# Groups in pairs with all batches inside a pair, in a grouped attention on one Trainium2 core

## The reference

```python
def _div_clamp_fp8(x, scale):
    y = jnp.clip(x.astype(jnp.float32) / scale, -FP8_MAX, FP8_MAX)
    y = y.astype(jnp.bfloat16).astype(jnp.float32)
    return _fp8_roundtrip(y)
...
ln_out = _ln(hidden_states, ln_w, ln_b)
q = _ln(_fp8_linear_pertensor(ln_out, wq, wq_scale, q_in_scale).reshape(b, s, g, hpg, d), qln_w, qln_b)
k = _ln(_fp8_linear_pertensor(ln_out, wk, wk_scale, k_in_scale).reshape(b, s, g, d), kln_w, kln_b)
v = _fp8_linear_pertensor(ln_out, wv, wv_scale, v_in_scale).reshape(b, s, g, d)
core = _gqa(q, k, v).reshape(b, s, nh * d)
qx = _ln(_fp8_linear_pertensor(ln_out, wqx, wqx_scale, qx_in_scale).reshape(b, s, g, hpg, d), qxln_w, qxln_b)
kx, vx = jnp.split(jnp.einsum('bsi,oi->bso', cond, w_kv_x), 2, axis=-1)
...
xout = _gqa(qx, kx, vx).reshape(b, s, nh * d)
catq = _div_clamp_fp8(jnp.concatenate([core, xout], axis=-1), proj_smooth)
return jnp.einsum('bsi,oi->bso', catq, wproj) * (proj_in_scale * proj_w_scale)
```

## Time and profile before

| | us |
|---|---|
| median of 3 runs (lowest, highest) | 987.29 (986.53, 988.27) |
| the profiled execution: its own time | 992.78 |
| its span | 991.0 |
| PE busy | 921.8 (93%) |
| DVE busy | 748.4 (76%) |
| ACT busy | 585.3 (59%) |
| POOL busy | 490.0 (49%) |

### The profile page before, as it was taken

One profiled execution on the slowest core, in us unless ns is written; L12 is line 12 of the kernel. 1 busy time (PEld: TensorE's weight loads), 2 busy tenths in 40 slices (PEclk: granted clock), 3 DMA queues, 4 the chain that ended last, 5 costly groups with the idle time before them and its releaser, 6 DMA issues. The chain is left out here.

```text
span 991.0 us, 17524 instructions
## 1 busy us (share of the span) xinstructions
PE 921.8 (93%) x5677; PEld 739.2 (75%) x5677; DVE 748.4 (76%) x2035; ACT 585.3 (59%) x1711; POOL 490.0 (49%) x409
## 2 busy tenths in 40 slices
PE   7999999998889988996889999999999999999988
PEld 6455656665768655664678899988999889999976
DVE  6764564433785778998899889789887898788785
ACT  1753444437435778864664766756766667766743
POOL 3265667652124223434666565475664755645650
PEclk9998999999999989997999999999999999999999
DMA  9725212214101200000020100101002010000201
GB/s 320 285 87 222 78 67 86 75 75 184 47 1 62 86 2 2 3 22 0 22 64 1 32 13 2 65 1 44 1 1 65 1 43 1 4 20 2 97 1 43
DMA packets 19657, 55.18 MB, mean 56 GB/s; under 512 B 3264, under 2 KB 9488, under 8 KB 19056
## 3 DMA queue, kind: packets, MB, share of 16 engines
q1 hardware_dynamic: 13968, 40.68, 11.4%
q0 software_dynamic: 4512, 12.33, 3.6%
q10 hardware_dynamic: 1088, 1.05, 0.3%
HBM read 45.78 MB, written 8.26 MB: 55 GB/s over the span
## 5 line engine op out<-in xcount | busy, mean ns | idle before, releaser
L2513 ACT ACTIVATE y<-bank,g_mx 128x256 f32<-128x256 f32 x256 | 117.2, 484 | 115.6 <-DVE g_mx L2696 115.6
L2797 POOL TENSOR_TENSOR y<-y,g_sm 128x1024 f32<-128x1024 f32 x64 | 119.9, 1893 | 25.3 <-DVE g_sm L2712 25.3
L2773 POOL TENSOR_TENSOR g_c<-arena 128x1024 fp32r<-128x1024 f32 x30 | 64.0, 2132 | 112.4 <-DVE arena L2617 112.4
L2386 PE MATMUL bank<-arena 128*128 128x256 f32 x512 | 116.3, 380 | 0.0
L2386 PEld LDWEIGHTS bank<-arena 128*128 128x128 f32 x512 | 94.9, 190 | 12.0 <-issue 0.2
L767 PE MATMUL bank<-arena 128*128 x188 | 90.0, 602 | 0.0
L2269 PE MATMUL bank<-cst,y 128*128 128x128 f32 x512 | 71.9, 274 | 10.9 <-POOL y L2797 6.3
L2696 DVE TENSOR_REDUCE g_mx<-bank 128x2 f32<-128x512 f32 x128 | 79.2, 675 | 0.2 <-PE bank L2386 0.2
L1105 DVE TENSOR_SCALAR arena<-bank 128x256 f32<-128x256 f32 x47 | 19.9, 423 | 76.5 <-PE bank L767 68.1
L2363 PE MATMUL bank<-g_qh,g_xs 128*128 128x256 f32 x256 | 66.8, 298 | 7.0 <-POOL g_xs L2747 6.8
L2305 PE MATMUL bank<-g_ph,g_c 128*128 128x256 f32 x248 | 65.9, 304 | 4.0 <-ACT y L2513 2.3
(11 more groups left out here) (427 smaller groups left out, 2656.2 us busy)
## 6 DMA issues: line engine op xcount, KB each, us to landing
arena<-in_dram SPq DMA_DIRECT2D x16, 768.0 KB, 15.4
arena<-in_dram SPq DMA_DIRECT2D x21, 512.0 KB, 3.7
arena<-b_pairs SPq DMA_DIRECT2D x8, 512.0 KB, 7.4
arena<-in_dram SPq DMA_DIRECT2D x3, 1024.0 KB, 5.0
arena<-in_dram SPq DMA_DIRECT2D x2, 704.0 KB, 5.6
x<-in_dram SPq DMA_DIRECT2D x4, 256.0 KB, 5.1
cx<-in_dram SPq DMA_DIRECT2D x4, 256.0 KB, 5.3
cxT<-in_dram SPq DMA_DIRECT2D x4, 256.0 KB, 5.8
```

What stands on the lines that cost most here:

```text
L2386: m = pe.matmul(o[:, st * 256:st * 256 + 256], g_t[:, c, st * P:st * P + P], keys, start=True, stop=True)
L2513: m = act.activation(g_p[:, c, st, :], o[:, st * 256:st * 256 + 256], ACT.Exp, bias=g_mx[j % 2][:, 2 * c + st:2 * c + st + 1], accum_out=g ...
L2773: pool.tensor_tensor(cat, g_o[j % 2], g_om, ALU.subtract).then_inc(s_gc, 1)
L2797: pool.tensor_tensor(pf, pf, sums, ALU.mult).then_inc(s_gp, 1)
```

## The change

The order of items becomes pairs of groups: items 0 to 7 are (g0, b0), (g1, b0), (g0, b1), (g1, b1), and so on, so that keys and values are projected in every even iteration, two buffers hold them in place of four, and batches finish one after the other in the last pair. The raw query weights get places of their own: the second group's are loaded and centred in the mLSTM stage already, later ones wait in part of yT and of the arena. The preparation for the next pair stands at iterations 5 to 8 of a pair: centring of the even group at the end of 5, of keys and of the odd group at the end of 6, the even group's splits at the end of 7 (ACT's high parts at its start, with those of keys and values), the low parts of keys and values early in the first iteration of the new pair, the odd group's splits at its end, and the projection's splits in the fourth and fifth. Roundings of batches 1 to 3 move to the ends of iterations 0 to 4. One buffer holds the quantised output in place of two. In the last layer, batches 0 and 1 are normalised in iterations 29 to 32, and PE does their transposes and logits around the last items; the lists of the feed-forward are reordered to match. Arena addresses shift by 48.

The diff, cut to its core:

```diff
                 if s_ == 3:
                     split_w_dve(dve, 0, BOTH)
+                    centre_w_dve(dve, V, 1)
...
+        PAIR = 2 * B
+        G_OF = [2 * (j // PAIR) + j % 2 for j in range(NG)]
+        B_OF = [j % PAIR // 2 for j in range(NG)]
...
-        g_o = [yT[:, i, :] for i in range(2)]
-        g_f = [arena[:, at_:at_ + 1024] for at_ in (19456, 11264, 18432, 16384)]
+
+        def g_o(j):
+
+            return yT[:, 1, :] if j == NG - 1 else yT[:, 0, :]
...
-        kv_at = [(arena[:, 35792:36304], arena[:, 36304:36816]), (arena[:, 36816:37328], arena[:, 37328:37840]),
-                 (kv_more[:, 0:512], kv_more[:, 512:1024]), (arena[:, 37840:38352], arena[:, 26624:27136])]
-        g_k, g_v = ([kv_at[b][n].rearrange("p (t g d) -> p t g d", t=2, g=2) for b in range(B)] for n in range(2))
+        kv_at = [(arena[:, 35840:36352], arena[:, 36352:36864]), (kv_more[:, 0:512], kv_more[:, 512:1024])]
...
-                   1: (("G", "yt", 3),) + CROSS[3]}
+        G_AHEAD = {0: CROSS[1]}
+        G_EXTRA = {0: (("F", "t", 2), ("F", "o", 2)) + CROSS[2][0:3] + (("F", "t", 3), CROSS[2][3], ("F", "o", 3)) + CROSS[3],
+                   1: (("G", "yt", 2), ("G", "yt", 3)),
...
-            at_ = 35792 if g == 0 else (13312, 15360)[g % 2]
-            return arena[:, at_:at_ + 1024].rearrange("p (k n) -> p k n", k=KD)
+            if g < 2:
+                raw = (arena[:, 35840:36864], kv_more[:, :])[g]
+            else:
+                raw = (yT[:, 1, :], arena[:, 26624:27648])[g % 2]
+            return raw.rearrange("p (k n) -> p k n", k=KD)
...
-            at_ = 36816 if p == 0 else 14336
-            return arena[:, at_:at_ + 1024].rearrange("p (k n) -> p k n", k=KD)
+            return arena[:, 36864:37888].rearrange("p (k n) -> p k n", k=KD)
...
             sp.dma_start(g_pr(0), wp_d[0]).then_inc(s_gwp, 16)
-            sp.wait_ge(s_gx, 12)
-            sp.dma_start(g_qr(1), wq_d[1]).then_inc(s_gw, 16)
-            sp.wait_ge(s_gx, 16)
+            sp.wait_ge(s_gx, 8)
+            sp.wait_ge(s_gwp, 16)
             sp.dma_start(g_pr(1), wp_d[1]).then_inc(s_gwp, 16)
-            for g in range(2, G):
-                last = B * (g - 2) + B - 1
-                take(sp, ("G", "q", last, 1))
-                sp.dma_start(g_qr(g), wq_d[g]).then_inc(s_gw, 16)
-                if g % 2 == 0:
-                    take(sp, ("G", "kv", last, 1))
-                    sp.dma_start(g_kr(g // 2), wkv_d[g // 2]).then_inc(s_kvw, 16)
-                take(sp, ("G", "pj", last))
-                sp.dma_start(g_pr(g), wp_d[g]).then_inc(s_gwp, 16)
+            for p in range(1, G // 2):
+                if p == 1:
+                    sp.wait_ge(s_gv1, 32)
+                else:
+                    sp.wait_ge(s_gwl, 4 * (2 * p - 1))
+                sp.dma_start(g_qr(2 * p), wq_d[2 * p]).then_inc(s_gw, 16)
+                if p == 1:
+                    sp.wait_ge(s_gx, 16)
+                else:
+                    sp.wait_ge(s_kvl, 4 * p)
+                    sp.wait_ge(s_gwl, 4 * (2 * p))
+                sp.dma_start(g_kr(p), wkv_d[p]).then_inc(s_kvw, 16)
+                sp.wait_ge(s_gw, 16 * (2 * p + 1))
+                sp.dma_start(g_qr(2 * p + 1), wq_d[2 * p + 1]).then_inc(s_gw, 16)
+                for g in (2 * p, 2 * p + 1):
+                    take(sp, ("G", "pj", PAIR * p - 2 + g % 2))
+                    sp.wait_ge(s_gwp, 16 * g)
+                    sp.dma_start(g_pr(g), wp_d[g]).then_inc(s_gwp, 16)
...
                 G_pv(pe, j, a, o)
+            H_logits_pe(pe, 1)
+            H_column_pe(pe, 0)
             o = claim(pe, ("G", "pj", j - 1))
             pe.wait_ge(s_gc, j)
             G_pj(pe, j - 1, o)
+            yt_pe(pe, K_H, "H", (2,))
...
                 if i < NG:
-                    g, b = i // B, i % B
...
                     if i == 0:
                         keep_busy(pe, claim(pe, ("G", "q", 0, 0)), 6)
                     if b == 0:
                         pe.wait_ge(s_gwl, 4 * (g + 1))
-                        if g % 2 == 0:
-                            pe.wait_ge(s_kvl, 4 * (g // 2 + 1))
-                    if i < B:
-                        pe.wait_ge(s_gx, 4 * i + 4)
+                    if i < PAIR and i % 2 == 0:
...
                     cross_v_pe(pe, 2, g_wvx[:, 0, :], g_wvx[:, 1, :], (3,))
                     F_o_pe(pe, 3)
+                    cross_v_pe(pe, 3, g_wvx[:, 0, :], g_wvx[:, 1, :])
                 if i == 1:
-                    yt_pe(pe, K_G, "G", (3,))
-                    cross_v_pe(pe, 3, g_wvx[:, 0, :], g_wvx[:, 1, :])
+                    yt_pe(pe, K_G, "G", HIGH)
+            yt_pe(pe, K_H, "H", LOW)
+            pe.wait_ge(s_hwr, 1)
+            H_logits_pe(pe, 0)
             G_end_pe(pe)
...
-                    G_scale_act(act, 2)
+                if 0 < i < NG - 1 and i % PAIR == PAIR - 1:
+                    take(act, ("G", "q", i - 1, 1))
+                    split_w_act(act, G_OF[i + 1], BOTH)
+                    split_kv_act(act, G_OF[i + 1] // 2, BOTH)
+                if 0 < i < NG and i % PAIR == 0:
+                    take(act, ("G", "q", i - 1, 1))
+                    split_w_act(act, G_OF[i + 1], BOTH)
...
                 if i == 0:
                     split_p_act(act, 0)
+                    cross_v_act(act, 3)
                 if i == 1:
-                    G_scale_act(act, 3)
-                    cross_v_act(act, 3)
-                if i == 3:
-                    act.wait_ge(s_gx, 16)
-                    split_w_act(act, 1, BOTH)
-                if B <= i < NG - B and 1 <= i % B < 3:
-                    split_w_act(act, i // B + 1, (i % B - 1,))
-                    if i // B % 2:
-                        split_kv_act(act, i // B // 2 + 1, (i % B - 1,))
-                if i < NG - B and i % B == 3:
-                    split_p_act(act, i // B + 1)
+                    G_scale_act(act, 2)
+                    G_yt_act(act, 3)
+                if i in (2, 3):
+                    G_scale_act(act, 3, ((0, 1), (2, 3))[i - 2])
+                if i == 3 or PAIR <= i < NG and i % PAIR in (2, 3):
+                    split_p_act(act, 2 * (i // PAIR) + i % PAIR - 2)
+            H_yt_act(act, 0)
+            H_yt_act(act, 1)
             G_end_act(act)
...
             j = NG - 1
             G_add_dve(dve, j - 2)
+            have(dve, ("G", "pj", j - 2))
+            ln_open_batch(dve, V, 2)
             for c in G_PT_DVE:
                 G_pt_dve(dve, j, c)
             have(dve, ("G", "pv", j - 1, 0))
             have(dve, ("G", "pv", j - 1, 1))
             dve.wait_ge(s_gc, j - 1)
             G_ob_dve(dve, V, j - 1, g_om)
+            ln_scale(dve, K_H, 2)
             for a in range(2):
                 have(dve, ("G", "pv", j, a))
                 G_ob_dve(dve, V, j, h_om, slice(512 * a, 512 * a + 512))
-            have(dve, ("G", "pj", j - 2))
-            ln_open_batch(dve, V, 1)
-            ln_scale(dve, K_H, 0)
             G_add_dve(dve, j - 1)
-            have(dve, ("G", "pj", j - 1))
-            ln_open_batch(dve, V, 2)
-            ln_scale(dve, K_H, 1)
+            dve.wait_ge(s_hc, 32)
+            H_compare_dve(dve, 0)
             G_add_dve(dve, j)
             have(dve, ("G", "pj", j))
             ln_open_batch(dve, V, 3)
-            ln_scale(dve, K_H, 2)
             ln_scale(dve, K_H, 3)
...
                         G_pt_dve(dve, i - 2, 0)
-                if i == B:
-                    dve.wait_ge(s_gx, 16)
-                    split_w_dve(dve, 1, BOTH)
-                if B <= i < NG - B and i % B == 1:
-                    centre_w_dve(dve, V, i // B + 1)
-                    if i // B % 2:
-                        centre_k_dve(dve, V, i // B // 2 + 1)
-                if B <= i < NG - B and 2 <= i % B < 4:
-                    split_w_dve(dve, i // B + 1, (i % B - 2,))
-                    if i // B % 2:
-                        split_kv_dve(dve, i // B // 2 + 1, (i % B - 2,))
-                if 0 < i < NG and i % B == 0:
-                    split_p_dve(dve, i // B)
+                if 0 < i < NG and i % PAIR == 0:
+                    split_kv_dve(dve, i // PAIR, BOTH)
+                if i == 4 or PAIR <= i < NG and i % PAIR in (3, 4):
...
                 if i == 0:
+                    split_w_dve(dve, 1, BOTH)
                     F_add_dve(dve, V, 2)
                     ln_open_batch(dve, V, 2)
                     G_round_dve(dve, V, 1, (0,))
-                    ln_scale(dve, K_G, 2)
-                    G_round_dve(dve, V, 1, (1,))
                     F_add_dve(dve, V, 3)
                     ln_open_batch(dve, V, 3)
+                    ln_scale(dve, K_G, 2)
                     split_p_dve(dve, 0)
-                    ln_scale(dve, K_G, 3)
-                if i == 2:
-                    centre_w_dve(dve, V, 1)
+                if 1 <= i < 5:
+                    G_round_dve(dve, V, 2 + (i - 1) // 2, ((i - 1) % 2,))
```

(67 more changed lines are left out.)

152 lines of the change are left out of this document (75 added, 77 removed).

## The result

The changed kernel takes 998.49 us (median of 4 runs, 996.49 to 1000.91) against 987.78 for the kernel before: ratio 1.0104, 95% interval 1.0081 to 1.0127. It is slower, by 10.7 us in the medians and 10.3 (1.04%) by the ratio, where +3.0 was forecast; 998.49 lies above the range.

A forecast was written before the change was run, and what follows sets the result against it. PE bounds even groups, a DVE, ACT and POOL chain odd ones. Prologue 0, first boundary's last step +1.46, two boundaries +0.4 each, tail +0.8: +3.0 on the median 987.29, so 990.3 us; range 980 to 996.

The forecast's parts named there:

- splits that POOL holds at the pair boundaries: Iterations 7 and 8: POOL's product delays DVE's weight splits by 1.25; a boundary costs 4.93 against 4.5 today, +0.4.
- roundings that give the prologue back: First iterations: q of iteration 2 starts 6 earlier, but DVE's spread roundings return the whole gain by iteration 8, net 0.
- PE's floor: Product layer's attention: PE's busy time, 13.59 us an iteration in the last odd group, 15.49 in an even one.
- A: Pair boundaries and roundings: POOL does not hold DVE's splits and roundings, −6.3, 981 us; chance 0.18.
- B: Pair boundaries and roundings: the hold is partial, half the price (0.65) stays, −1.7, 985.6 us; chance 0.20.
- D: Product layer's loop: nothing is held and the excess of 5.7, 4.5 and 4.5 goes, 975 us; chance 0.04.
- C: Prologue: q of iteration 2 gains 2 in place of 6, the roundings' cost remains, 994 us; chance 0.16.
- about 6 lower: Pair boundaries: what the forecast sum would be lower by if POOL did not hold the splits.
- the tail: Last layer's end: early normalisation and logits of batches 0 and 1 delay the last quantisation 2.2; taken as +0.8.
- bound of +2.5: Last layer's end: upper limit of the tail's cost, if all of the delay passes on; the lower was −1.0.
- less stands in the queues behind it: Last layer's end: reason given for the last batch's scaling coming only some 0.8 later.
- the early stage: mLSTM stage: centring the second group's weights (1.4) fits DVE's idle 2.07, so costs nothing; 1.4 at most without it.

The follow-up runs named there:

- second pair: Both kernels profiled once more, unchanged: the kernel before took 988.56 us, the changed kernel 1000.77, each a single run.
- Run 4: Changed kernel with DVE's weight splits moved from the ends of iterations 7 and 8 to behind the next iteration's add and copy: 989.06 us, ratio 1.0022.
- run 7: Changed kernel with five extra matmuls of constants, unused, in PE's idle time near the end: 994.99 us, ratio 1.0066.
- Run 1: Changed kernel with POOL centring the second group's weights ahead of the mLSTM copies, not behind them: 996.38 us, ratio 1.0095.
- run 3: Changed kernel with ten extra matmuls of constants, unused, in PE's idle time near the end: 997.36 us, ratio 1.0098.

## Why the prediction was right or wrong

**Direction: right; loop: the mechanism right, its sum in part by luck.** The forecast was slower, by splits that POOL holds at the pair boundaries and roundings that give the prologue back. The hold was put at 1.25 and measures 1.32 (2.98 − 1.66). Iterations 6, 7 and 8 exceed PE's floor by 0.54, 2.60 and 1.44, where 0.69, 2.78 and 1.46 stood; at the later boundaries the first of these is 0.14. Beside POOL's centring one instruction of the quantisation (L2645) takes 1.23 in place of 0.42, 0.8 where 1.0 was taken, at the first boundary as at the later ones; what else makes the later ones shorter isn't shown. Counted from the first q matmul, iteration 2 starts at 44.2 (42.8 forecast), 4 at 78.6 (76.2), 8 at 143.4 (142.1). So iteration 8 is 1.3 later than in the kernel before, where the forecast had 0, and what follows it costs 1.1, where 2.3 stood: the sum of 2.4 for 2.3 is two misses that cancel. In the second pair they are 2.6 and 0.9. Run 4 shows the reason of the boundaries' price, not only its size: the same splits 1.3 us later in DVE's list are still awaited by PE, and cost 2.7 us less a boundary without the hold. Rivals A, B and D are out by L2251 at 1.79. C, the missing gain of the prologue, is not all wrong: iteration 2 comes 4.8 us earlier than before in the first pair and 3.3 in the second, between C's 2 and the forecast's 6. That without a hold the time would be "about 6 lower" disagrees with the prediction's own rival A, which makes it 9.3.

**The step that failed: the tail, "+0.8", with its bound of +2.5.** It measured +5.2. The chain of quantisations was followed, though under its size: the last one ends 2.9 later where 2.2 stood, and the last batch's scaling (L293) follows 1.4 later where 0.8 stood. These are its rows, before and then changed, 40.3 and 41.8 us after the q matmul of iteration 31:

```profile
964.92 0.74 DVE L293 TENSOR_SCALAR arena<-x,mv,rs 128x256 f32<-128x256 f32 x2 [0.60 <-POOL rs L333]
```

```profile
964.86 0.73 DVE L293 TENSOR_SCALAR arena<-x,mv,rs 128x256 f32<-128x256 f32 x2 [1.14 <-POOL rs L333]
```

The step priced DVE's opening of batch 2, but no hold of the early scalings: those of batches 1 and 2 have an instruction of 1.98 and 2.22 in place of 0.4 beside POOL's products, which is the loop's own mechanism (before, the quantisation itself had the second of these holds). What failed above all was the sentence that less stands in the queues behind it, counted as a gain. The work removed there was what kept PE at 2.4 GHz while the last layer norm was made. Without it PE waits 2.61 us and does the rest of the ranking at 1.2 GHz, 3.6 us by run 7: from the end of that scaling to the end of the span the changed kernel takes 29.1 us, run 7 25.5 and the kernel before 25.3. The bound treated PE's durations as fixed, which the earlier trace rows are only at the clock at which they were taken.

**The second step that failed: the early stage, "nothing".** It measured 2.0, and 1.6 in the second pair. DVE's part fits the idle time as the step says. POOL's part was not followed through POOL's own list: the subtractions stood behind copies that wait for DVE until 375, and then held DVE, by the very mechanism that the loop's working used. Run 1 shows the place to be the cause, since some 15 us earlier, in POOL's idle time, they cost nothing.

The sum with the measured terms, 2.4 + 2.0 + 5.2, gives 9.6 for the forecast 3.0. With the tail at its bound of 2.5 it would be 6.9, inside the range; the range's upper end, 996.0, fell with that bound.

## What to carry to other kernels

DVE work with two operands in SBUF, and the roundings and scalings that were held here with one, go where POOL is not in a long product; instructions that read a bank can stand beside it, so swapping the two in the list may be worth more than the change around them (8 us here). Work that is moved ahead of a chain's end leaves a hole at its old place: look at what PE does there, since a wait may halve its clock for what follows, and the moved work delays what it is put ahead of. A moved step is followed on every engine's list, the idle ones too.

## What the runs showed of the hardware

- PE after an idle time: after 1.31 us the mLSTM matmuls kept 0.94 a group. After 2.83 us the same group took 1.64 and 1.56 in two of six profiles and 0.94 in four; the granted clock fell to 0.50 in five of the six, in three of them only behind the group, and not at all in run 3. At the end, 2.61 us of idle time was followed by 10 us at a granted clock of 0.52, 0.51, 0.70 and 0.66 in four profiles.
- Extra matmuls that compute nothing, 2.40 us of them in that hole, brought 3.6 us in the trace; 4.56 us of them brought 1.9.
- A POOL product of 128x1024 holds a DVE instruction with two SBUF inputs (0.47 to 1.79) and one with a single bf16 input (0.42 to 1.79) until about its end, and leaves those that read an operand from a bank (0.74 and 0.68). Not every DVE instruction that reads SBUF alone is held: the sum over the keys' weights (L2224, a TENSOR_REDUCE at 556.84 in the changed kernel) takes 0.67 in the midst of such a product, as elsewhere.
